# Edge tiles cut at 128 nodes in place of 256, in a graph kernel of three EdgeConv layers and one relational layer

## The chip, the core and the metric

The kernel runs on one core of a Trainium2 chip. TensorE multiplies matrices (PE in the profile, its weight loads PEld), VectorE (DVE) and ScalarE (ACT) work elementwise, GpSimd (POOL) issues indirect DMAs here, SyncE (SP) issues the plain ones. The metric is the device time of one execution in microseconds.

## The reference

A graph of N = 12500 nodes with 128 features and E = 212500 edges (100000 random pairs in both directions and a loop at each node), sorted by their target `dst`. Three EdgeConv layers run one after the other, with a ReLU after the first two:

```python
m = concatenate([x[dst], x[src] - x[dst]])
h = relu(m @ W1 + b1) @ W2 + b2          # one row per edge
x = segment_max(h, dst)                  # -inf becomes 0
```

Then `x = layernorm(x_in + x)`, a relational layer (for each node and each of 8 edge types the mean of the neighbours' rows, times that type's 128x128 matrix, summed over the types, ReLU), and a second residual layernorm.

## The kernel before

`x[dst] @ (W1a - W1b) + b1` is a table in SBUF (`table`, one 128-column block for each 128 nodes, 98 blocks), and `x[src] @ W1b` is a table in DRAM (`tab_b`). An edge needs the sum of one row of each.

**Tiles.** The edges, sorted by target, are cut into tiles of at most 128 edges. A tile never crosses the border of a block of nodes, so each block ends with a tile that is partly empty. In the kernel before a block has 256 nodes (`W2P`, 49 blocks, `NS`), and the number of tiles is a compile-time bound: (E + 49 x 127) / 128 rounded up to a multiple of 16, NT = 1712. Four tiles (`GT`) are a group: 428 groups (`NG`) in each layer, in bodies of eight (`LG`): 53 bodies and a rest of four groups (`OV`). The setup counts the edges of each block, finds each tile's block and first edge, and stores for each tile the target of each edge inside the block (`row_two`), the source (`idx_all`), and the column at which a node's run of edges ends (`col_end`).

**One group** goes through the engines so, eight groups deep on POOL and SP, two deep on the others:
- SP loads `locs` and `cuts` of the group, broadcast to 128 partitions (256 KB, L618).
- POOL gathers the four tiles' source rows from `tab_b`, one indirect DMA a tile (L834). It waits until TensorE is through with the group eight earlier (`s_p1`).
- ScalarE reads the tiles' block numbers and copies each tile's part of `table`, 128x256, to a fixed place (L1270).
- VectorE makes two one-hot matrices of `locs`, against the lanes 0 to 127 (L1564) and 128 to 255 (L1566).
- TensorE, for each tile: a transpose of the gathered rows (L966) and two float32 products of the table's halves with the one-hots, accumulated (L968, two passes each, so four matmuls in the profile). Then W2 for the group before (L975) and four transposes for the one before that (L990).
- ScalarE evicts with ReLU (L1279). VectorE runs a segmented running maximum over the 512 edges of a group (L1593); ScalarE evicts its transposed result (L1291), and SP stores it to `scan_rows` (256 KB, L627).

In layer 0 the position of each node's last edge is found as well: VectorE makes one-hots of the end columns (L1585), TensorE multiplies them with a two-column `lanes` that tells lower from upper half (L982), VectorE collects (L1598). After the last group `end_rows` turns this into `endrow`: comparisons with the tiles' blocks (L1606), two steps on 128x1792 for each half (L1609, L1614), transposes (L1000) and a copy (L1328) for each half, and matmuls that sort by block (L1005). Between layers POOL gathers each node's last row of `scan_rows` by `endrow` (L813), and the tables of the next layer are made.

Beside layer 1's groups VectorE sorts all edges by (source, type), bitonically, with a few passes over 128x2048 between two steps (L1672 and L1673, L1677 and L1678); beside layer 2's it ranks them and cuts them into tiles of the relational stage, and POOL fetches windows. These extra pieces are written into the loops by body number. The relational stage has its own tiles (427 groups, blocks of 256 nodes), gathers from `z_tab` (L891), and is not touched.

Where POOL waits:

```python
for k in range(many):
    at = Lt(l, i, k)
    if at.j == 0:
        pool.wait_ge(s_idx[at.h], at.n + 1)
    pool.wait_ge(s_p1, at.G + 1)
    tick()
    for t in range(GT):
        g.indirect_dma_start(rows[k][:, t, :], None, tab_b, ...
```

Of the kernel before, what the change touches and what calls it, by code (L numbers as in the profile page):

```python
# [24 lines left out]
F32 = mybir.dt.float32  # L25
I32 = mybir.dt.int32
# [19 lines left out]
def gnn_kernel(nc, x, src, dst, etype, params, w_rel, out):  # L46
# [9 lines left out]
    NT = -(-((E + NS * (P - 1)) // P) // HT) * HT  # L56
# [26 lines left out]
    assert NB % CB == 0 and NB + 1 <= P and NB % 2 == 0 and NG % HG == 0 and NG % 2 == 0 and 2 <= OV <= HG  # L83
# [18 lines left out]
    with ExitStack() as ctx:  # L102
# [14 lines left out]
        pidx_up = sb("pidx_up", [P, 1])  # L117
        lane_f = sb("lane_f", [P, 1])
# [37 lines left out]
        thr_row = a.cut(NST)  # L156
        thr_col = a.cut(1, F32, NST)
        jbase = a.cut(NQ)
        full = a.cut(LC * NST).rearrange("p (c b) -> p c b", c=LC)
        cnt0 = a.cut(1, F32, NST)  # L160
        win_at = a.cut(1, I32, NST)
        win_i = a.cut(P, I32, NST)
        win_f = a.cut(P, F32, NST)
        cnt1 = a.cut(1, F32, NST)
        start = a.cut(1, F32, NST)
        step_mat = a.cut(P)
        upto_mat = a.cut(P)
        deg_b = a.cut(1, F32, NS)
        nt_i = a.cut(1, I32, NS)
        nt_f = a.cut(1, F32, NS)  # L170
        upto = a.cut(1, F32, NS)
        shift2 = a.cut(2, F32, NS)
        iota_j = a.cut(NTP, F32, NS)
        past = a.cut(NTP, F32, NS)
# [49 lines left out]
        end_up = a.cut(HT)  # L224
        end_lo = [a.cut(HT) for _ in range(2)]
        lanes = [a.cut(2 * HT, BF16).rearrange("p (t f) -> p t f", f=2) for _ in range(2)]
# [4 lines left out]
        hot_t = [a.cut(2 * GT * P).rearrange("p (h e) -> p h e", h=2) for _ in range(2)]  # L231
        tabs = [a.cut(GT * W2P).rearrange("p (t n) -> p t n", n=W2P) for _ in range(2)]
# [3 lines left out]
        end_at = a.cut(2 * NTP).rearrange("p (f t) -> p f t", f=2)  # L236
        row_base = a.cut(NTP)
        row_t = a.cut(2 * NTP).rearrange("p (f t) -> p f t", f=2)
        blk_hot = a.cut(NQ * NS).rearrange("p (q b) -> p q b", b=NS)
# [149 lines left out]
        s_lane = sem("s_lane")  # L389
# [52 lines left out]
        PV_CONST = 14  # L442
# [336 lines left out]
        def _(pool):  # L779
# [8 lines left out]
            g.iota(thr_row, [[W2P, NST]], base=0, channel_multiplier=0, **exact).then_inc(s_gp, 1)  # L788
            g.iota(thr_col, [[0, 1]], base=0, channel_multiplier=W2P, **exact).then_inc(s_gp, 1)
# [111 lines left out]
        def _(pe):  # L901
# [5 lines left out]
            for c in range(LC):  # L907
                last = mm(ps[0:NST, 0, 0:1], full[:, c, :], ones[:, :], start=(c == 0), stop=(c == LC - 1))
# [1194 lines left out]
```

## Time and profile before

| | |
|---|---|
| time, median of 3 runs | 9480.66 us (9475.42 to 9495.2) |
| the profiled execution | 9484.52 us, span 9482.7 us |
| PE busy | 6710.9 us, 71% |
| PEld busy | 5255.2 us, 55% |
| DVE busy | 5275.8 us, 56% |
| ACT busy | 4898.1 us, 52% |
| POOL busy | 6935.8 us, 73% |
| mean granted TensorE clock | 0.909 |

The three edge layers fill the span from about 145 to 7050 us, the relational stage from about 7286 to the end. A group of instructions is named by its line in the kernel before. Issuing a DMA counts as busy on POOL. The mean of a group of instructions hides where the long ones are, and an engine can be busy for a large share and still always have time in hand: what an engine waited for, and for how long, is read beside it.

### The profile page before, as it was taken

The page shows a single profiled execution, that of the slowest core. Times are in us where ns is not written, and L with a number is a line of the kernel's source. Part 1 is how long each engine was busy: PE and PEld are TensorE (multiplying, and loading weights), DVE is VectorE, ACT ScalarE, POOL GpSimd, SP SyncE. Part 2 cuts the span into 40 slices and gives each one's busy share as a digit, 9 for nine tenths or more (in the row PEclk, how much of TensorE's full clock was granted, in tenths as well). Part 3 has the DMA queues.
Part 4 walks back from the last instruction along what each step waited for, and adds up shares of the span by engine and source line. Part 5 has one row for each costly group of instructions (what it writes and reads, how often), then busy time and mean ns, then how long its engine had stood idle before and what let it go on. Part 6 is the DMA issues. An engine that isn't in the chain of part 4 may idle for free. (4 is left out here: it accounts for less than half of the span.)

```text
span 9482.7 us, 160130 instructions
## 1 busy us (share of the span) xinstructions
PE 6710.9 (71%) x41098; PEld 5255.2 (55%) x41098; DVE 5275.8 (56%) x9611; ACT 4898.1 (52%) x11866; POOL 6935.8 (73%) x7196
## 2 busy tenths in 40 slices
PE   6777777876677777777667777777768555555555
PEld 5666666665565565666555666666654343333333
DVE  5666666665577666666546555555556333333334
ACT  2444444443344444444434444444446777777776
POOL 4777777776777777777777777777764777777775
PEclk9999999998899999999989999999999777777777
DMA  5665656664455555565545666656656222222222
GB/s 144 158 158 157 158 158 158 157 159 126 127 151 148 153 154 153 148 149 149 151 125 147 166 161 162 164 157 157 159 154 248 54 54 54 54 54 54 54 54 67
DMA packets 896156, 1259.78 MB, mean 133 GB/s; under 512 B 185847, under 2 KB 601079, under 8 KB 895270
## 3 DMA queue, kind: packets, MB, share of 16 engines
q1 hardware_dynamic: 650494, 784.23, 27.0%
q0 software_dynamic: 230048, 471.99, 22.6%
q10 hardware_dynamic: 15408, 0.88, 0.1%
q8 instruction: 121, 1.98, 0.1%
q14 instruction: 85, 0.70, 0.0%
HBM read 834.14 MB, written 424.01 MB: 133 GB/s over the span
## 5 line engine op out<-in xcount | busy, mean ns | idle before, releaser
L834 POOL DMA_INDIRECT agg<-tab_b,agg x5136 | 4984.5, 971 | 1596.2 <-issue 1527.3
L968 PE MATMUL ps<-tab_a 128*128 128x128 f32 x20544 | 3080.0, 284 | 3.4 <-issue 3.4
L968 PEld LDWEIGHTS ps<-tab_a 128*128 128x128 f32 x20544 | 2874.6, 202 | 4.1 <-issue 4.0
L966 PE MATMUL ps<-ident,agg 128*128 128x128 f32 x5136 | 1480.8, 288 | 1588.6 <-DMA agg<-tab_b,agg 1503.0
L1593 DVE TENSOR_TENSOR_SCAN agg<-agg,ps 128x512 f32<-128x512 bf16 x1284 | 1639.4, 1277 | 1689.8 <-PE ps L975 1687.7
L1279 ACT ACTIVATE agg<-ps 128x512 f32<-128x512 f32 x1284 | 766.8, 597 | 3475.2 <-PE ps L968 3442.3
L891 POOL DMA_INDIRECT work<-z_tab,work x1708 | 1611.6, 944 | 576.0 <-issue 501.3
L1163 PE MATMUL ps<-tab_a,work 128*128 128x256 f32 x3416 | 1228.0, 522 | 914.7 <-DMA work<-z_tab,work 611.6
L966 PEld LDWEIGHTS ps<-ident,agg 128*128 128x128 f32 x5136 | 753.1, 147 | 1824.6 <-issue 1420.3
L1270 ACT ACTIVATE tab_a<-tab_a 128x256 f32 x5136 | 1713.7, 404 | 52.6 <-issue 41.5
L1163 PEld LDWEIGHTS ps<-tab_a,work 128*128 128x128 f32 x3416 | 841.5, 258 | 1301.3 <-DVE tab_a L2038 1108.2
L2038 DVE TENSOR_TENSOR tab_a<-ps,tab_a 128x256 f32 x1708 | 724.3, 424 | 1416.4 <-PE ps L1163 1230.8
L975 PE MATMUL ps<-agg,w 128*128 128x512 f32 x2568 | 1342.0, 605 | 0.0
L1356 ACT ACTIVATE tab_a<-tab_a,work 128x256 f32<-128x256 f32 x1708 | 883.6, 588 | 467.0 <-PE ps L1163 453.4
L1564 DVE SCALAR_TENSOR_TENSOR tab_a<-agg,pidx,ps 128x512 f32<-128x512 bf16 x1284 | 932.6, 726 | 42.1 <-ACT agg L1279 42.0
L1566 DVE SCALAR_TENSOR_TENSOR tab_a<-agg,pidx_up,ps 128x512 f32<-128x512 bf16 x1284 | 950.0, 740 | 0.0
L990 PEld LDWEIGHTS ps<-ident,agg 128*128 128x128 f32 x5136 | 609.8, 141 | 468.0 <-issue 463.2
L990 PE MATMUL ps<-ident,agg 128*128 128x128 f32 x5136 | 786.5, 276 | 2.5 <-DVE agg L1593 2.3
L1347 ACT ACTIVATE tab_a<-work 128x256 f32<-128x256 f32 x1708 | 727.4, 496 | 62.5 <-ACT tab_a L1356 6.3
L1291 ACT ACTIVATE agg<-ps 128x512 f32<-128x512 f32 x1284 | 739.3, 576 | 16.9 <-PE ps L990 11.5
L1585 DVE TENSOR_SCALAR agg<-iota_b,agg 128x128 bf16<-128x128 bf16 x1712 | 332.9, 271 | 490.3 <-PE ps L982 473.0
L813 POOL DMA_INDIRECT work<-scan_rows,endrow x294 | 288.6, 982 | 197.5 <-issue 99.7
(252 smaller groups left out, 2982.0 us busy)
## 6 DMA issues: line engine op xcount, KB each, us to landing
agg<-row_two SPq DMA_DIRECT2D x1284, 256.0 KB
scan_rows<-agg SPq DMA_DIRECT2D x1284, 256.0 KB
agg<-tab_b,agg POOLq DMA_INDIRECT x5136
z_tab<-tab_a SPq DMA_DIRECT2D x84, 512.0 KB, 3.7
work<-z_tab,work POOLq DMA_INDIRECT x1708, 2.5
tab_b<-work SPq DMA_DIRECT2D x42, 448.0 KB, 3.1
work<-in_x SPq DMA_DIRECT2D x26, 448.0 KB, 5.6
z_tab<-work SPq DMA_DIRECT2D x14, 512.0 KB, 3.9
```

The costliest lines, as they stand in the source:

```text
L834: g.indirect_dma_start(rows[k][:, t, :], None, tab_b, bass.IndirectOffsetOnAxis(ap=idx[at.h][:, at.j * GT + t:at.j * GT + t + 1], axis=0)) ...
L891: g.indirect_dma_start(got[k % LG][:, t, :], None, z_tab, bass.IndirectOffsetOnAxis(ap=meta_of(k, 0, t).bitcast(I32), axis=0)).then_inc(s_ ...
L966: mm(to, rows[at.k][:, t, :], ident[:, :], is_transpose=True, start=True, stop=False)
L968: last = mm(to, tabs[at.s][:, t, h * P:(h + 1) * P], hot_t[at.s][:, h, t * P:(t + 1) * P], start=False, stop=(h == 1))
L975: mm(ps[:, 2 + at.s, :], w2[:, l], h1[at.s], start=True, stop=True).then_inc(s_p2, 1)
L990: last = tr(ps[:, 4 + at.s, t * P:(t + 1) * P], scan[at.s][:, t * P:(t + 1) * P], ident[:, :])
L1163: last = mm(flat[:, to:to + W2P], got[k % LG][:, t, :], hot_r[k % 4][:, t, :], start=True, stop=True)
L1270: last = a_(tabs[s][:, t, :], table[:, bass.ds(blk[t] * W2P, W2P)], ACT.Copy)
L1356: last = a_(hot_r[k % 4][:, t, :], off_r[k % 2][:, t, :], ACT.Relu, scale=meta_of(k, 3, t), bias=meta_of(k, 2, t))
L1564: v.scalar_tensor_tensor(out=hot_t[at.s][:, 0, :], in0=locs[at.k], scalar=pidx[:, 0:1], in1=ps[:, at.s, :], op0=ALU.is_equal, op1=ALU.bypass)
L1566: v.scalar_tensor_tensor(out=hot_t[at.s][:, 1, :], in0=locs[at.k], scalar=pidx_up[:, 0:1], in1=ps[:, at.s, :], op0=ALU.is_equal, op1=ALU.b ...
L1593: v.tensor_tensor_scan(scan[at.s], cuts[at.k], ps[:, 2 + at.s, :], scan[1 - at.s][:, GT * P - 1:GT * P], ALU.min, ALU.max).then_inc(s_scan, 1)
```

## The change

A block has 128 nodes in the edge layers: 98 blocks, and 99 with the end mark. The bound on tiles becomes (E + 98 x 127) / 128 rounded up to a multiple of 16, NT = 1760, 440 groups, 55 bodies and no rest. A target inside its block is now below 128, so one one-hot a group and one float32 product (two matmuls) a tile remain, and ScalarE copies 128x128 a tile. In layer 0 the end marks need one column instead of two, the operations that split the lanes go, and `end_rows` loses its loop over the halves. The setup's operands have 98 or 99 entries in place of 49 or 50. The relational stage keeps blocks of 256.

The core of the diff:

```diff
-    NT = -(-((E + NS * (P - 1)) // P) // HT) * HT
+    NT = -(-((E + NB * (P - 1)) // P) // HT) * HT
...
-        hot_t = [a.cut(2 * GT * P).rearrange("p (h e) -> p h e", h=2) for _ in range(2)]
-        tabs = [a.cut(GT * W2P).rearrange("p (t n) -> p t n", n=W2P) for _ in range(2)]
+        hot_t = [a.cut(GT * P) for _ in range(2)]
+        tabs = [a.cut(GT * P).rearrange("p (t n) -> p t n", n=P) for _ in range(2)]
...
                         mm(to, rows[at.k][:, t, :], ident[:, :], is_transpose=True, start=True, stop=False)
-                        for h in range(2):
-                            last = mm(to, tabs[at.s][:, t, h * P:(h + 1) * P],
-                                      hot_t[at.s][:, h, t * P:(t + 1) * P], start=False, stop=(h == 1))
+                        last = mm(to, tabs[at.s][:, t, :], hot_t[at.s][:, t * P:(t + 1) * P], start=False, stop=True)
...
-                        last = mm(ps[:, 6 + at.h, 2 * col:2 * col + 2], ends[at.s][:, t, :], lanes[at.h][:, col, :],
-                                  start=True, stop=True)
+                        last = mm(ps[:, 6 + at.h, col:col + 1], ends[at.s][:, t, :], lane1[:, :], start=True, stop=True)
...
-                for f in range(2):
-                    for q in range(NQ):
-                        at = f * 2048 + q * P
-                        last = tr(flat[:, at:at + P], end_at[:, f, q * P:(q + 1) * P], ident[:, :])
-                    last.then_inc(s_et, 1)
+                for q in range(NQ):
+                    last = tr(flat[:, q * P:(q + 1) * P], end_at[:, q * P:(q + 1) * P], ident[:, :])
+                last.then_inc(s_et, 1)
                 pe.wait_ge(s_er, 3)
-                for f in range(2):
-                    for q in range(NQ):
-                        last = mm(ps[:, 7, 256 + f * NS:256 + (f + 1) * NS], row_t[:, f, q * P:(q + 1) * P],
-                                  blk_hot[:, q, :], start=(q == 0), stop=(q == NQ - 1))
+                for q in range(NQ):
+                    last = mm(ps[:, 7, 256:256 + NB], row_t[:, q * P:(q + 1) * P], blk_hot[:, q, :],
+                              start=(q == 0), stop=(q == NQ - 1))
...
-                    last = a_(tabs[s][:, t, :], table[:, bass.ds(blk[t] * W2P, W2P)], ACT.Copy)
+                    last = a_(tabs[s][:, t, :], table[:, bass.ds(blk[t] * P, P)], ACT.Copy)
...
-                    for f in range(2):
-                        act.wait_ge(s_et, f + 1)
-                        last = a_(row_t[:, f, :], flat[:, f * 2048:f * 2048 + NTP], ACT.Copy)
-                    last.then_inc(s_er, 3)
+                    act.wait_ge(s_et, 1)
+                    a_(row_t, flat[:, 0:NTP], ACT.Copy).then_inc(s_er, 3)
...
-                    v.scalar_tensor_tensor(out=hot_t[at.s][:, 0, :], in0=locs[at.k], scalar=pidx[:, 0:1],
-                                           in1=ps[:, at.s, :], op0=ALU.is_equal, op1=ALU.bypass)
-                    v.scalar_tensor_tensor(out=hot_t[at.s][:, 1, :], in0=locs[at.k], scalar=pidx_up[:, 0:1],
-                                           in1=ps[:, at.s, :], op0=ALU.is_equal, op1=ALU.bypass).then_inc(s_hot, 1)
+                    v.scalar_tensor_tensor(out=hot_t[at.s], in0=locs[at.k], scalar=pidx[:, 0:1], in1=ps[:, at.s, :],
+                                           op0=ALU.is_equal, op1=ALU.bypass).then_inc(s_hot, 1)
...
-                            v.tensor_scalar(end_up, end_c[at.h], float(P), -float(P), ALU.is_ge, ALU.mult
-                                            ).then_inc(s_lane, 1)
-                            for f, side in enumerate((ALU.is_lt, ALU.is_ge)):
-                                v.tensor_scalar(lanes[at.h][:, :, f], end_c[at.h], float(P), lane_f[:, 0:1], side, ALU.mult)
-                            dve.wait_ge(s_lane, 2 * at.H + 1)
-                            tick()
-                            v.tensor_tensor(end_lo[at.h], end_c[at.h], end_up, ALU.add).then_inc(s_lane, 1)
-                            dve.wait_ge(s_lane, 2 * at.H + 2)
-                            tick()
...
-                    last = v.tensor_scalar(blk_hot[:, q, :], iota[:, 0:NS], blk_col[:, q:q + 1], None, ALU.is_equal)
+                    last = v.tensor_scalar(blk_hot[:, q, :], iota[:, 0:NB], blk_col[:, q:q + 1], None, ALU.is_equal)
...
-                for f in range(2):
-                    last = v.scalar_tensor_tensor(out=row_t[:, f, :], in0=end_at[:, f, :], scalar=0.0, in1=row_base,
-                                                  op0=ALU.is_gt, op1=ALU.mult)
-                last.then_inc(s_ec, 1)
+                v.scalar_tensor_tensor(out=row_t, in0=end_at, scalar=0.0, in1=row_base, op0=ALU.is_gt, op1=ALU.mult
+                                       ).then_inc(s_ec, 1)
```

## Rows read from the trace of the kernel before

**Rows 1.** The page, part 1: busy us of each engine, share, instructions.

```profile
PE 6710.9 (71%) x41098; PEld 5255.2 (55%) x41098; DVE 5275.8 (56%) x9611; ACT 4898.1 (52%) x11866; POOL 6935.8 (73%) x7196
```

**Rows 2.** Windows over L834, one a layer: us, POOL busy, granted clock, DMA share, GB/s.

```profile
144.60:2282.90 2138.30, 1616.71 (x1712) 0.98 0.61 157
2462.20:4710.50 2248.30, 1726.78 (x1712) 0.96 0.57 151
4863.80:7045.10 2181.30, 1641.02 (x1712) 0.96 0.60 158
```

**Rows 3.** Timeline in layer 0: start, us, engine, line, operation [idle before, releaser].

```profile
1002.31 0.30 PE L966 MATMUL ps<-ident,agg 128*128 128x128 f32 x1 [1.33 <-DMA agg<-tab_b,agg]
...
1002.89 0.27 PE L966 MATMUL ps<-ident,agg 128*128 128x128 f32 x1
...
1002.90 0.94 POOL L834 DMA_INDIRECT agg<-tab_b,agg  x1 [0.30 <-issue]
1003.00 0.61 PE L968 MATMUL ps<-tab_a 128*128 128x128 f32 x4
...
1003.45 0.27 PE L966 MATMUL ps<-ident,agg 128*128 128x128 f32 x1
...
1004.15 0.94 POOL L834 DMA_INDIRECT agg<-tab_b,agg  x1 [0.30 <-issue]
...
1005.52 0.64 PE L990 MATMUL ps<-ident,agg 128*128 128x128 f32 x4
```

**Rows 4.** Waits of the whole run: us in total, times, longest.

```profile
ACT agg L1279 <- PE ps L968: 3442.3, 1269, 12.6
...
PE ps L966 <- DMA agg<-tab_b,agg: 1503.0, 1005, 16.1
...
POOL agg L834 <- PE ps L968: 37.2, 122, 0.3
```

**Rows 5.** The page, part 5: two costly groups with count, busy us, mean ns.

```profile
L1270 ACT ACTIVATE tab_a<-tab_a 128x256 f32 x5136 | 1713.7, 404 | 52.6 <-issue 41.5
...
L1566 DVE SCALAR_TENSOR_TENSOR tab_a<-agg,pidx_up,ps 128x512 f32<-128x512 bf16 x1284 | 950.0, 740 | 0.0
```

**Rows 6.** Timeline after layer 0's last gather: the end rows.

```profile
2292.52 2.25 DVE L1606 TENSOR_SCALAR work<-iota,blk_col 128x49 f32<-128x49 f32 x14
...
2294.69 3.95 DVE L1609 SCALAR_TENSOR_TENSOR work<-work 128x1792 f32<-128x1792 f32 x2
...
2302.68 5.43 PE L1000 MATMUL ps<-ident,work 128*128 128x128 f32 x28 [9.64 <-DVE work L1614]
...
2308.22 1.66 ACT L1328 ACTIVATE work<-ps 128x1792 f32<-128x1792 f32 x1 [0.58 <-PE ps L1000]
...
2309.93 11.64 PE L1005 MATMUL ps<-work 128*128 128x49 f32 x56 [1.82 <-ACT work L1328]
...
2323.12 0.94 POOL L813 DMA_INDIRECT work<-scan_rows,endrow  x1 [40.22 <-DVE endrow L1622]
```

**Rows 7.** Layer 1: timeline, then by source line: duration min/median/max ns, first and last start.

```profile
3007.24 1.20 DVE L1677 TENSOR_TENSOR work<-work 128x1024 f32<-128x1024 f32 x1
3007.44 1.82 POOL L834 DMA_INDIRECT agg<-tab_b,agg  x1 [0.31 <-issue]
...
L1672 DVE TENSOR_TENSOR work<-work x110: 658/676/1117, 2535.4 to 2981.5; 128x512 f32<-128x512 f32 x110
...
L1677 DVE TENSOR_TENSOR work<-work x116: 1194/1200/1250, 2999.0 to 4566.2; 128x1024 f32<-128x1024 f32 x116
```

**Rows 8.** The relational stage: L891 by source, and a window (PE, PEld, DVE, ACT, POOL).

```profile
L891 POOL DMA_INDIRECT work<-z_tab,work x1708: 940/944/957, 7285.9 to 9416.8; - x190
...
8000.00:8200.00 200.00, 114.58 (x320) 78.59 (x320) 68.90 (x163) 150.56 (x324) 151.24 (x161) 0.77 0.21 54
```

**Rows 9.** Timeline at the start of layer 2's groups: TensorE.

```profile
4874.06 0.45 PE L966 MATMUL ps<-ident,agg 128*128 128x128 f32 x1 [15.75 <-DMA agg<-tab_b,agg]
...
4875.15 0.42 PE L966 MATMUL ps<-ident,agg 128*128 128x128 f32 x1
```

More of the change, by code:

```diff
@@ L82, in gnn_kernel @@
     assert N + SRC_OFF + P < 16000 and N <= 1 << 14 and R <= 8
-    assert NB % CB == 0 and NB + 1 <= P and NB % 2 == 0 and NG % HG == 0 and NG % 2 == 0 and 2 <= OV <= HG
+    assert NB % CB == 0 and NB + 1 <= P and NB % 2 == 0 and NG % HG == 0 and NG % 2 == 0 and OV in (0, HG)
     TAIL = ERP * P + P - E
@@ L155, in gnn_kernel @@
         last_f = a.cut(LC)
-        thr_row = a.cut(NST)
-        thr_col = a.cut(1, F32, NST)
+        thr_row = a.cut(NBT)
+        thr_col = a.cut(1, F32, NBT)
         jbase = a.cut(NQ)
[L159 to L165, printed above, removed]
+        full = a.cut(LC * NBT).rearrange("p (c b) -> p c b", c=LC)
+        cnt0 = a.cut(1, F32, NBT)
+        win_at = a.cut(1, I32, NBT)
+        win_i = a.cut(P, I32, NBT)
+        win_f = a.cut(P, F32, NBT)
+        cnt1 = a.cut(1, F32, NBT)
+        start = a.cut(1, F32, NBT)
         step_mat = a.cut(P)
         upto_mat = a.cut(P)
[L168 to L174, printed above, removed]
+        deg_b = a.cut(1, F32, NB)
+        nt_i = a.cut(1, I32, NB)
+        nt_f = a.cut(1, F32, NB)
+        upto = a.cut(1, F32, NB)
+        shift2 = a.cut(2, F32, NB)
+        iota_j = a.cut(NTP, F32, NB)
+        past = a.cut(NTP, F32, NB)
         blk_f = a.cut(NQ)
@@ L223, in gnn_kernel @@
         ends = [a.cut(GT * P, BF16).rearrange("p (t n) -> p t n", n=P) for _ in range(2)]
[L224 to L226 removed]
         a = Area(tab_a, TAB)
         table = a.cut((NB + 2) * P)
[L231 to L232 removed]
+        hot_t = [a.cut(GT * P) for _ in range(2)]
+        tabs = [a.cut(GT * P).rearrange("p (t n) -> p t n", n=P) for _ in range(2)]
         a = Area(work, WORK)
[L236 removed]
+        end_at = a.cut(NTP)
         row_base = a.cut(NTP)
[L238 to L239 removed]
+        row_t = a.cut(NTP)
+        blk_hot = a.cut(NQ * NB).rearrange("p (q b) -> p q b", b=NB)
         no_edge = a.cut(NB)
@@ L907, in _ @@
             for c in range(LC):
-                last = mm(ps[0:NST, 0, 0:1], full[:, c, :], ones[:, :], start=(c == 0), stop=(c == LC - 1))
+                last = mm(ps[0:NBT, 0, 0:1], full[:, c, :], ones[:, :], start=(c == 0), stop=(c == LC - 1))
             last.then_inc(s_pt, 1)
             pe.wait_ge(s_pv, PV_START)
-            mm(ps[0:NS, 1, 0:1], step_mat[0:NST, 0:NS], start, start=True, stop=True).then_inc(s_pt, 1)
+            mm(ps[0:NB, 1, 0:1], step_mat[0:NBT, 0:NB], start, start=True, stop=True).then_inc(s_pt, 1)
             pe.wait_ge(s_pv, PV_TILES)
-            mm(ps[0:NS, 2, 0:1], upto_mat[0:NS, 0:NS], nt_f, start=True, stop=True).then_inc(s_pt, 1)
+            mm(ps[0:NB, 2, 0:1], upto_mat[0:NB, 0:NB], nt_f, start=True, stop=True).then_inc(s_pt, 1)
             pe.wait_ge(s_pv, PV_PAST)
@@ L1584, in step @@
                             col = at.j * GT + t
-                            last = v.tensor_scalar(ends[at.s][:, t, :], iota_b[:, :], end_lo[at.h][:, col:col + 1], None,
+                            last = v.tensor_scalar(ends[at.s][:, t, :], iota_b[:, :], end_c[at.h][:, col:col + 1], None,
                                                    ALU.is_equal)
```

49 lines of the change are left out of this document (19 added, 30 removed).

## The prediction

> **What bounds the kernel now.** I began with the page's busy times [rows 1]. POOL has the largest sum and it issues two things only: gathers of rows by index in the three edge layers (L834) and in the relational stage (L891), beside a few at layer ends. TensorE is close behind, so the shares alone do not decide it. The windows over L834, one for each layer from its first gather to its last, do [rows 2]. In layer 0 1712 gathers take 2138.3 us, which is 1.249 us for each, or 4.996 us for a group of four tiles. Layer 1 takes 2248.3 us and layer 2 2181.3 us for the same count. The timeline of one group [rows 3] shows what such an interval is: 0.94 us busy and 0.30 us between two gathers, and the next begins 1.25 us after the last. TensorE in the same stretch stood idle 1.33 us until the gathered rows landed, then worked. The waits say it for the whole run [rows 4]: TensorE waited 1503.0 us for these landings in 1005 places, ScalarE waited 3442.3 us for TensorE, while POOL was held back by TensorE for 37.2 us in 122 places, none over 0.3 us, which is its usual 0.30 us between two gathers. So in the edge layers POOL sets the pace, and TensorE, ScalarE and VectorE all have slack: of its 5.0 us a group takes TensorE about 3.85 us (1002.31 to 1006.16 in rows 3).
>
> **What the change does to each part.** Tiles per layer go from 1712 to 1760, groups from 428 to 440. The three fixed numbers of gathers follow the tiles, whatever the data.
>
> *Term 1, 48 more gathers in each of three layers.* The added groups carry the same four gathers as the others. 48 x 1.249 = 60.0 us in a layer, 179.9 us in three. Nothing hides it, since POOL is the engine that everybody waits for. Each added group also brings its 256 KB load and its 256 KB store on SP's queue; the DMA share is about 0.6 in these windows [rows 2] and the rate per us does not change, so I add nothing for them.
>
> *Term 2, work taken from TensorE, ScalarE and VectorE inside the loops.* Per tile two of four L968 matmuls go. The pitch of a tile is 0.56 us, of which 0.11 us is the transpose's lead (1002.89 to 1003.45 and 1003.00 in rows 3), so the other 0.45 us halves: 0.22 us a tile, 0.89 us a group. VectorE loses one one-hot of 0.74 us a group [rows 5], and in layer 0 the small operations that split the end lanes. ScalarE's copies become half as wide; a 128x128 copy is not in the trace, its cost lies between nothing and the 0.40 us of the 128x256 one [rows 5], and I need no value, because ScalarE waits for TensorE anyway. All of it stands beside POOL's 5.0 us and is worth nothing while the gathers last longer. If that cover were gone these 0.89 us would count; rival A prices it.
>
> *Term 3, the drain after a layer's last gather.* Here no gather follows, and the last group's matmuls are on the path to the store for which the next stage waits. 0.89 us shorter, three times: -2.7 us. Bounds 0 and -5 (two groups' worth and the one-hot).
>
> *Term 4, the end rows after layer 0* [rows 6]. POOL idles 40.2 us here, so every step counts. The 14 comparisons of L1606 go from 49 to 98 columns: 2.25 us now, between 2.25 and 4.5 us then; I take 2.95, +0.7, a third of the way. The two pairs of 1792-column operations (3.95 us for the pair of L1609, and L1614's is like it) become single ones: -3.95. 28 transposes become 14. ScalarE copies their halves one after the other, and the matmuls wait for the second copy, begun at 2308.22 and done at 2309.88; the first, of the same length, begins when half of the 5.43 us and an end of 0.6 us are over, at about 2306.0, and is done at 2307.6: -2.3. The 56 matmuls of L1005 (49 columns, 11.64 us, 0.208 each) become 28 of 98 columns. The nearest row is L1000 with 128 columns in 5.43 / 28 = 0.194, so width costs little there: 28 x 0.208 = 5.8, -5.8 (bounds -5.8 and 0). Sum of the term -11.3 us, bounds -4 and -12.
>
> *Term 5, the sort beside layer 1.* Layer 1 is 110.0 us longer than layer 0 [rows 2], and its POOL busy time is longer by the same 110.1 us (1726.8 against 1616.7), so the gathers themselves last longer. The timeline shows where [rows 7]: VectorE runs a pair of min and max passes over 1024 columns, and the gather that begins inside takes 1.82 us in place of 0.94. There are 55 stages of four shorter passes (L1672 x110 with its partner) and 116 pairs (L1677, L1678). Neither count changes. What a stage costs hangs on where in the gather it starts. From the gathers beside the first of these pairs at 2999.0 us to the last at 4566.2 us, the 116 pairs lose 0.71 us each; starts from 0.15 to 0.30 us after a gather's start lose about 0.05, those 1.1 us after it over 1.5. The passes follow the scan, the scan follows TensorE, and TensorE follows the landing, so the cut of 0.89 us moves all starts. The starts are spread now and I expect them spread then: evenly spread they would lose 0.64 and 0.38 us where they lose 0.71 and 0.42, so -8 and -2: -10 us. The bounds are wide, -110 (none collides) and +70 (most begin at the worst place); both ends would need the starts to lock onto one point. Of the 43 us that layer 2 has over layer 0, 24 are gathers made longer in the same way by the ranking work and the rest eight steps in which POOL fetches windows; no change.
>
> The Trainium skill states this collision as a lock: "SBUF — State Buffer", section "SBUF: two separate sides", has a port pair shared by VectorE and GpSimd that one holds for a whole instruction while the other blocks, for VectorE passes with two SBUF inputs too. The trace agrees (1.82 us in rows 7 against 0.94 in rows 3). By this rule the removed one-hots, which read one operand from PSUM, would free nothing, and the sum stays as it is.
>
> *Term 6, the setup.* 13 comparisons get 99 columns for 50, some small operands 98 or 99 partitions for 49, two small VectorE operations go. VectorE waits for loads around them; 0, bounds -1 and +3.
>
> **Sum.** 179.9 - 2.7 - 11.3 - 10 = +155.9 us. The profiled execution took 9484.5 us for a span of 9482.7: 9640.4. The median of the runs lies 3.9 us below it: 9636.5.
>
> **Rivals.**
>
> A. TensorE is what sets the pace (the other side). If POOL were led by TensorE through the eight buffers, a group would fall from 4.996 us by 0.89 to 4.11 us: 1320 x 4.11 = 5425 us and the 153 us of extra in layers 1 and 2, against 6567.9 us now, so 9484.5 - 990 - 14 = about 8480 us. It decides as soon as a group falls under 4.87 us, where the 12 more groups are paid. For it speaks that TensorE is busy 71% of the span [rows 1]. Against it: the 1005 waits for landings, no wait of POOL above its 0.30 us [rows 4], and the relational stage, where gathers of another table beside other matmuls have the same 0.94 us and the same pace, 161 in 200 us [rows 8]. 3%.
>
> B. The gather itself becomes cheaper with fewer operations of the others beside it. To come out even 156 us in 5280 gathers are needed, 30 ns each of 1249; the time would be about 9480. Against it: a minimum of 940 ns and a median of 944 in the relational stage, where VectorE is busy a third of the time [rows 8], and the same median in the edge layers, so that the other engines seem to cost the gathers nothing outside the sort. 1%.
>
> C. TensorE's clock. Its granted clock is 0.96 to 0.98 in the edge layers [rows 2] and 0.77 in the relational stage [rows 8]. With a quarter of the work taken from it, TensorE waits longer for rows in each group, and the clock will fall to somewhere between. In a stretch at 1.2 GHz, just after 15.75 us of idling, a tile takes 1.09 us in place of 0.56 [rows 9]. A group needs 3.85 - 0.89 = 2.96 us at 2.4 GHz, and 5.9 at most at 1.2, against POOL's 5.0. So it decides only when the granted clock of a whole layer falls under 2.96 / 5.0 = 0.59; at 0.77 a group takes 3.8 us and nothing is lost. At 0.55 it would take 5.4 us, 1320 x 0.39 = 510 us more: about 10,150. 3%.
> The Trainium skill's page "TensorE: Matmul & The Clock Gate", section "HAM oscillation — how this bites in real kernels", speaks against the change here: bursts with waits for DMA between them fall back to half the clock each time. By it alone every group would run at 1.2 GHz and the time go to rival C's; the relational stage, where TensorE waits for gathers too, keeps 0.77 [rows 8], and I go by that.
>
> D. The sort's starts lock. At the two bounds of term 5 the time would be 9537 or 9717 us. For it speaks that all of it is periodic; against it that the delays themselves shift the phase. 5%.
>
> **How the numbers follow.** The forecast, POOL's pace with 48 more gathers a layer, has 88%. The range 9590 to 9675 is 9637 with most of what term 5 leaves open, the rest of the terms together being good for some 10 us. A measurement of this kernel tells 0.2% (19 us) from no change. Forecast, C and D are slower, 96%; B is no change, 1%; A is faster, 3%.
>
> **What would show it.** The L834 windows: 1760 gathers in about 2198 us in layer 0, 2298 in layer 1, 2241 in layer 2, with the median gather still at 0.94 us. TensorE's waits for landings grow by some 1000 us, ScalarE's remain. L968 has 10,560 matmuls. POOL's idle time ahead of the first L813 falls from 40 us to about 28. The granted clock in the edge layers is between 0.77 and 0.96. A layer 0 window under 2180 us, or POOL waiting for TensorE, would make the forecast wrong.

## The result and the profile after

The changed kernel takes 9645.1 us (median of 4, 9638.7 to 9649.7) against 9482.1 us (median of 4), a ratio of 1.017 with a 95% interval of 1.0152 to 1.0187: 163 us slower. 9637 was forecast. Its profiled execution took 9645.8 us, span 9643.9, 161.2 us more than the span before.

The page after, part 1, to be read beside [rows 1], and from part 5 the groups of the gathers and of TensorE's product:

```profile
PE 6280.8 (65%) x31480; PEld 4638.4 (48%) x31480; DVE 4439.2 (46%) x8018; ACT 4500.4 (47%) x12090; POOL 7060.5 (73%) x7340
...
L828 POOL DMA_INDIRECT agg<-tab_b,agg x5280 | 5109.6, 968 | 1645.6 <-issue 1597.4
...
L961 PE MATMUL ps<-tab_a 128*128 128x128 f32 x10560 | 2278.4, 318 | 4.8 <-issue 4.8
```

The same two groups before:

```profile
L834 POOL DMA_INDIRECT agg<-tab_b,agg x5136 | 4984.5, 971 | 1596.2 <-issue 1527.3
...
L968 PE MATMUL ps<-tab_a 128*128 128x128 f32 x20544 | 3080.0, 284 | 3.4 <-issue 3.4
```

TensorE, VectorE and ScalarE all work less, by 430, 837 and 398 us. POOL works 125 us more, and the time follows POOL. The three windows over the gathers (now L828) have the columns of [rows 2]:

```profile
143.70:2342.40 2198.70, 1662.58 (x1760) 0.86 0.59 157
2513.60:4812.30 2298.70, 1762.53 (x1760) 0.85 0.57 151
4964.70:7204.00 2239.30, 1684.43 (x1760) 0.86 0.59 158
```

Layer 0: 2198.7 / 1760 = 1.249 us from one gather to the next, as before. A gather of layer 0 is busy 0.945 us on average (1662.58 / 1760) and was busy 0.944, so the removed one-hots, which read one operand from PSUM, freed nothing. Timeline in layer 0, the place of [rows 3]:

```profile
1000.93 0.94 POOL L828 DMA_INDIRECT agg<-tab_b,agg  x1 [0.30 <-issue]
1001.21 0.44 PE L960 MATMUL ps<-ident,agg 128*128 128x128 f32 x1 [3.29 <-DMA agg<-tab_b,agg]
...
1002.18 0.94 POOL L828 DMA_INDIRECT agg<-tab_b,agg  x1 [0.30 <-issue]
```

TensorE idles 3.29 us ahead of this group where it idled 1.33 us, and finds its clock lower: the transpose takes 0.44 us. Over the run (waits, columns of [rows 4]) its waits for landings grew from 1503 to 2063 us. POOL still idles about 0.30 us ahead of a gather, and in 5122 of 5280 cases (4910 of 5136 before) for "issue", which means nothing that the profile shows:

```profile
ACT agg L1267 <- PE ps L961: 3723.0, 1315, 17.7
...
PE ps L960 <- DMA agg<-tab_b,agg: 2062.6, 882, 21.4
POOL agg L828 <- issue: 1597.4, 5122, 21.6
```

The span, cut at POOL's first and last instruction of each stage (us), also for the experiments told below:

| stage | before | changed | e1 | e2 | e3 | e4 | e7 | e8 | e10 | e13 |
|---|---|---|---|---|---|---|---|---|---|---|
| setup | 144.6 | 143.7 | 142.8 | 145.7 | 145.8 | 144.3 | 144.3 | 143.7 | 145.3 | 143.2 |
| layer 0, gathers | 2138.3 | 2198.8 | 2198.8 | 2139.8 | 2200.9 | 2198.5 | 2199.0 | 2198.6 | 2261.8 | 2200.7 |
| end rows | 40.2 | 26.4 | 36.1 | 25.8 | 28.4 | 29.6 | 26.3 | 27.0 | 27.2 | 27.5 |
| tables for layer 1 | 139.1 | 144.8 | 145.5 | 138.6 | 145.5 | 146.0 | 138.3 | 141.8 | 144.5 | 147.1 |
| layer 1, gathers | 2248.3 | 2298.6 | 2322.4 | 2231.2 | 2283.5 | 2292.8 | 2281.0 | 2299.3 | 2308.8 | 2293.7 |
| border and tables for layer 2 | 153.3 | 152.4 | 154.3 | 153.8 | 154.0 | 156.2 | 155.1 | 153.4 | 151.4 | 154.9 |
| layer 2, gathers | 2181.3 | 2239.3 | 2239.5 | 2181.1 | 2240.7 | 2239.4 | 2241.9 | 2240.6 | 2294.5 | 2243.2 |
| border, up to relational | 240.8 | 242.9 | 248.2 | 242.4 | 244.4 | 243.9 | 243.4 | 243.6 | 244.5 | 243.2 |
| relational and end | 2196.8 | 2197.0 | 2197.7 | 2196.0 | 2196.2 | 2198.0 | 2195.5 | 2195.8 | 2198.1 | 2199.0 |

The changed kernel against before: +168.8 us in the three gather stages, -13.8 in the end rows, +5.7 in the tables for layer 1, the rest +0.5.

The end rows after the change (timeline, lines that answer to [rows 6]):

```profile
2352.15 2.62 DVE L1578 TENSOR_SCALAR work<-iota,blk_col 128x98 f32<-128x98 f32 x14
...
2354.68 2.02 DVE L1580 SCALAR_TENSOR_TENSOR work<-work 128x1792 f32<-128x1792 f32 x1
...
2358.81 3.25 PE L989 MATMUL ps<-ident,work 128*128 128x128 f32 x14 [6.12 <-DVE work L1583]
2362.16 1.66 ACT L1316 ACTIVATE work<-ps 128x1792 f32<-128x1792 f32 x1 [8.78 <-PE ps L989]
2363.87 3.37 PE L993 MATMUL ps<-work 128*128 128x98 f32 x28 [1.81 <-ACT work L1316]
...
2368.79 0.94 POOL L807 DMA_INDIRECT work<-scan_rows,endrow  x1 [26.35 <-DVE endrow L1589]
```

### The profile page after: what moved, and what is told of

Same layout as the page of the kernel before. It is cut to its first block and busy times, and to the rows that moved or that the text cites. A ratio compares the mean times of both kernels' runs of the same rounds, so it can differ in the third digit from the quotient of the medians.

```text
span 9643.9 us, 140435 instructions
## 1 busy us (share of the span) xinstructions
PE 6280.8 (65%) x31480; PEld 4638.4 (48%) x31480; DVE 4439.2 (46%) x8018; ACT 4500.4 (47%) x12090; POOL 7060.5 (73%) x7340
## 5 line engine op out<-in xcount | busy, mean ns | idle before, releaser
L828 POOL DMA_INDIRECT agg<-tab_b,agg x5280 | 5109.6, 968 | 1645.6 <-issue 1597.4
L960 PE MATMUL ps<-ident,agg 128*128 128x128 f32 x5280 | 1686.8, 319 | 2176.1 <-DMA agg<-tab_b,agg 2062.6
L1565 DVE TENSOR_TENSOR_SCAN agg<-agg,ps 128x512 f32<-128x512 bf16 x1320 | 1685.3, 1277 | 2310.1 <-PE ps L967 2308.2
L1267 ACT ACTIVATE agg<-ps 128x512 f32<-128x512 f32 x1320 | 788.1, 597 | 3733.2 <-PE ps L961 3723.0
L961 PE MATMUL ps<-tab_a 128*128 128x128 f32 x10560 | 2278.4, 318 | 4.8 <-issue 4.8
L960 PEld LDWEIGHTS ps<-ident,agg 128*128 128x128 f32 x5280 | 864.3, 164 | 2390.0 <-issue 1386.3
L961 PEld LDWEIGHTS ps<-tab_a 128*128 128x128 f32 x10560 | 1995.9, 235 | 5.6 <-issue 5.4
L967 PE MATMUL ps<-agg,w 128*128 128x512 f32 x2640 | 1660.8, 716 | 2.2 <-issue 2.2
L1258 ACT ACTIVATE tab_a<-tab_a 128x128 f32 x5280 | 1198.3, 297 | 63.0 <-issue 48.4
L981 PEld LDWEIGHTS ps<-ident,agg 128*128 128x128 f32 x5280 | 695.1, 154 | 605.7 <-issue 598.4
L1279 ACT ACTIVATE agg<-ps 128x512 f32<-128x512 f32 x1320 | 774.2, 587 | 319.1 <-PE ps L981 297.2
L981 PE MATMUL ps<-ident,agg 128*128 128x128 f32 x5280 | 880.0, 293 | 5.9 <-DVE agg L1565 3.8
L967 PEld LDWEIGHTS ps<-agg,w 128*128 128x128 f32 x2640 | 515.9, 243 | 2.4 <-issue 2.4
```

The source lines that it names most:

```text
L828: g.indirect_dma_start(rows[k][:, t, :], None, tab_b, bass.IndirectOffsetOnAxis(ap=idx[at.h][:, at.j * GT + t:at.j * GT + t + 1], axis=0)) ...
L960: mm(to, rows[at.k][:, t, :], ident[:, :], is_transpose=True, start=True, stop=False)
L961: last = mm(to, tabs[at.s][:, t, :], hot_t[at.s][:, t * P:(t + 1) * P], start=False, stop=True)
L967: mm(ps[:, 2 + at.s, :], w2[:, l], h1[at.s], start=True, stop=True).then_inc(s_p2, 1)
L981: last = tr(ps[:, 4 + at.s, t * P:(t + 1) * P], scan[at.s][:, t * P:(t + 1) * P], ident[:, :])
L1258: last = a_(tabs[s][:, t, :], table[:, bass.ds(blk[t] * P, P)], ACT.Copy)
```

## The experiments

**e1, e2: the number of tiles alone.** The kernel before with 1760 tiles, and the changed kernel with 1712 (this graph fills 1707 tiles at blocks of 128 and 1684 at 256).

```diff
 # e1, on the kernel before
-    NT = -(-((E + NS * (P - 1)) // P) // HT) * HT
+    NT = -(-((E + NB * (P - 1)) // P) // HT) * HT
...
 # e2, on the changed kernel
-    NT = -(-((E + NB * (P - 1)) // P) // HT) * HT
+    NT = -(-((E + NB // 2 * (P - 1)) // P) // HT) * HT
```

The rest of e1's edit lets ScalarE's loop end on 55 full bodies without a rest, as in the changed kernel.

> The kernel before (blocks of 256, two products a tile) with 1760 tiles a layer, the added 48 being empty. Theory (POOL's gathers set the pace): layer windows over the gathers of 2198, 2308 and 2241 us, the whole 180 us over before, about 9662. The changed kernel is then only 14 to 24 us faster than this one, by its end rows and little else. Rival (work saved on TensorE inside the loops was worth something in the changed kernel): this one is slower than the changed kernel by far more, up to 0.89 us in each of 1320 groups, 1175 us.

> The changed kernel with the number of tiles of before, 1712 (this graph fills 1707 tiles at blocks of 128, so nothing is cut off; for another graph the bound would not hold). Theory: windows of 2138, 2238 and 2180 us and a time 180 us under the changed kernel's, about 9465, so 0.1 to 0.3% under the kernel before. Rival (the empty tiles or the layer's border, not the number of gathers, cost the time): it stays above before.

e1 took 9679.2 us, ratio to before 1.0202 (1.0186 to 1.0217). e2 took 9458.2 us, ratio 0.9967 (0.9955 to 0.9978). Windows over the gathers, first of e1, then of e2:

```profile
142.80:2341.50 2198.70, 1662.61 (x1760) 0.98 0.61 157
2523.10:4845.50 2322.40, 1786.22 (x1760) 0.96 0.56 150
4999.80:7239.20 2239.40, 1684.48 (x1760) 0.96 0.60 158
```

```profile
145.70:2285.50 2139.80, 1618.39 (x1712) 0.86 0.59 157
2449.90:4681.10 2231.20, 1709.82 (x1712) 0.84 0.57 152
4834.90:7016.00 2181.10, 1641.00 (x1712) 0.85 0.59 158
```

Layers 0 and 2 are the same to 2 us in e1 and the changed kernel, and in e2 and before, though TensorE has half of the products in one of each pair. So the number of gathers makes the 60 us a layer, and in these two layers the work saved inside the loops is worth nothing. e1 came out 41 us over the changed kernel in the profiled spans (34 in the medians), where 14 to 24 were expected; 24 of it lie in layer 1, 10 in the end rows and 5 ahead of the relational stage. e2 is faster than both kernels, by 0.33% against before: 14 us from the end rows and 17 from layer 1's window. It holds only for graphs that fill no more than 1712 tiles.

**e3: TensorE's work put back.**

```diff
+                        mm(to, tabs[at.s][:, t, :], hot_t[at.s][:, t * P:(t + 1) * P], start=True, stop=True)
                         mm(to, rows[at.k][:, t, :], ident[:, :], is_transpose=True, start=True, stop=False)
```

> The changed kernel with each tile's product done twice, the first result overwritten, so TensorE has the matmuls of before again while VectorE, ScalarE and the number of tiles stay as changed. Theory: no change, 9640 to 9655, since TensorE works beside the gathers; the granted clock in the edge layers is back at 0.94 to 0.98. Rival (the lower clock of the changed kernel costs time somewhere): it comes out 5 us or more faster although it does more. Rival (TensorE's work counts): 1000 us slower.

It took 9636.3 us (9635.0 to 9641.2), ratio to before 1.0159 (1.0145 to 1.0173), with 10,560 matmuls more. Windows over the gathers of e3:

```profile
145.80:2346.70 2200.90, 1664.92 (x1760) 0.98 0.59 157
2520.60:4804.20 2283.60, 1747.59 (x1760) 0.97 0.57 152
4958.10:7198.90 2240.80, 1686.03 (x1760) 0.96 0.59 158
```

The granted clock is back at 0.96 to 0.98 from 0.85, and layers 0 and 2 do not move. Taken by itself the time of 9 us less would bear out the first rival, that the low clock costs something. The stages say otherwise: no border became shorter, layer 1's window did, by 15 us, and e7 has the same with the low clock. These 15 us lie in the 55 stages of four short passes of the sort: they lose 0.35 us each in e3 and 0.41 in e7, against 0.67 in the changed kernel and 0.57 when it ran again (e13), since they start at other places between two gathers. So neither TensorE's products nor its clock had a part in layers 0 and 2. In layer 1 the time hangs on where the sort's passes start, and code that does nothing (e7) moves that as much as TensorE's products do.

**e4: the sort's passes cut in two.**

```diff
-                    v.tensor_tensor(b_[:, :, 0, :], a_[:, :, 0, :], a_[:, :, 1, :], ALU.min)
-                    last = v.tensor_tensor(b_[:, :, 1, :], a_[:, :, 0, :], a_[:, :, 1, :], ALU.max)
+                    for part in range(2):
+                        if j < 10:
+                            half = SC >> (j + 2)
+                            of_, to_ = (x_[:, part * half:(part + 1) * half] for x_ in (a_, b_))
+                        else:
+                            half = 1 << (j - 1)
+                            of_, to_ = (x_[:, :, :, part * half:(part + 1) * half] for x_ in (a_, b_))
+                        v.tensor_tensor(to_[:, :, 0, :], of_[:, :, 0, :], of_[:, :, 1, :], ALU.min)
+                        last = v.tensor_tensor(to_[:, :, 1, :], of_[:, :, 0, :], of_[:, :, 1, :], ALU.max)
```

> The changed kernel with each of the 116 pairs of 1024-column passes of the sort beside layer 1 written as four passes of 512 columns. Theory (a gather waits for the end of the VectorE pass in progress): a stage then costs what the stages of four short passes cost, 0.42 us in place of 0.71, so layer 1's window falls by about 33 us to 2265, the time to 9612. Rival (a gather waits until the whole stretch of passes is over, or pays by the total time of passes): the window stays at 2298 or grows by a few us.

It took 9645.5 us, with layer 1's window at 2292.7 us: the expectation failed. The 116 stages lose 0.49 us each, as in the changed kernel (0.50). By the start's place they lose 0.1 to 0.5 us, and 1.2 us for starts about 0.55 us after a gather's start, where the long passes lose 0.36. The 55 stages of four short passes lose 1.3 us for starts there in the changed kernel (0.4 in before). That such a gather is held by more than one of the passes is my reading; no row shows which. Shorter passes lowered the worst case of the long ones (1.0 us in the last eighth of the table below, now 0.5) and brought one of their own.

**e10: what makes a VectorE operation hold up a gather.**

```diff
-                    v.scalar_tensor_tensor(out=hot_t[at.s], in0=locs[at.k], scalar=pidx[:, 0:1], in1=ps[:, at.s, :],
+                    v.scalar_tensor_tensor(out=hot_t[at.s], in0=locs[at.k], scalar=pidx[:, 0:1], in1=cuts[at.k],
                                            op0=ALU.is_equal, op1=ALU.bypass).then_inc(s_hot, 1)
```

> The changed kernel with one operand moved: the one-hot's second operand, whose value is not used, is read from the SBUF tile with the cuts in place of PSUM. Same operation, same length, same result. Theory (VectorE passes with two SBUF operands hold up the gathers): one 0.7 us pass a group now meets a gather in about half the cases and costs it 0.33 us on average, so each layer's window grows by 50 to 150 us and the gathers' busy time with it; the kernel comes to 9800 to 10,050. Rival (only the long stretches of the sort do it, by their length): no change, 9645.

It took 9778.0 us (one time; before took 9494.5 beside it). Windows over the gathers, then a one-hot with a gather beginning inside it:

```profile
145.30:2407.10 2261.80, 1725.61 (x1760) 0.84 0.56 153
2578.70:4887.50 2308.80, 1772.63 (x1760) 0.84 0.55 151
5039.00:7333.50 2294.50, 1739.53 (x1760) 0.84 0.55 154
```

```profile
1001.27 0.74 DVE L1549 SCALAR_TENSOR_TENSOR tab_a<-agg,pidx 128x512 f32<-128x512 bf16 x1
1001.61 1.22 POOL L828 DMA_INDIRECT agg<-tab_b,agg  x1 [0.30 <-issue]
```

Layer 0's gathers are busy 63.0 us longer and its window is 63.1 us longer (2198.7 and 1662.58 in the changed kernel). One operand moved from PSUM to SBUF did that, with the same operation and length: 706 of the layer's gathers overlap a one-hot, and they are 63.7 us longer in sum than at 0.944 us each, the 1054 others 0.5 us; in the changed kernel 623 gathers overlap one and are not longer at all. The effect is shown. Its size, 0.14 us a group, is under the 0.17 that I had reckoned, and the 9778 us lie just below the expected band, mainly because layer 1 grew by only 10 us, not 50 or more; why it did is open.

**e5, e6: three gathers a group.**

```diff
-                        for t in range(GT):
+                        for t in range(GT - 1):
                             g.indirect_dma_start(rows[k][:, t, :], None, tab_b,
...
-                    pe.wait_ge(s_rows[at.k], 64 * (at.n + 1))
+                    pe.wait_ge(s_rows[at.k], 48 * (at.n + 1))
...
-                        mm(to, rows[at.k][:, t, :], ident[:, :], is_transpose=True, start=True, stop=False)
+                        mm(to, rows[at.k][:, t % 3, :], ident[:, :], is_transpose=True, start=True, stop=False)
```

> The changed kernel with only three gathers a group; the fourth tile is computed from the rows of the first, so a quarter of the source rows is left out. It takes POOL's 5.0 us a group down to 3.75 and shows what stands behind it. Theory: TensorE needs about 3.0 us at full clock, so POOL still sets the pace, layer 0's window is 440 x 3.75 = 1650 us and the whole about 1600 us shorter, near 8050. Rival (TensorE at its lower clock is the next bound): a group stays above 3.9 us, the window above 1720.

> The kernel before with only three gathers a group, the fourth tile from the rows of the first (a quarter of the source rows left out). Theory: here TensorE's 3.85 us a group and its hand-overs come to the front, so layer 0's window is 428 x 3.9 to 4.3 us = 1670 to 1840 us, above that of the changed kernel with three gathers although it has 12 groups fewer: the work that the change saves is worth something only behind a faster gather. Rival (something other than TensorE and POOL is the next bound, the same in both): the window is 428 x 3.75 = 1605 us, 3% under the changed kernel's.

Both leave out a quarter of the source rows: the fourth tile takes the first one's. e5 took 7995.1 us, e6 7988.1 (one time each). Layer 0 in e5, then in e6 (us; PE, PEld, DVE, ACT, POOL busy; granted clock, DMA share, GB/s):

```profile
144.20:1794.50 1650.30, 1338.06 (x9630) 1004.02 (x9631) 1134.69 (x2740) 899.42 (x2735) 1248.21 (x1320) 0.95 0.70 192
```

```profile
142.50:1748.40 1605.90, 1586.07 (x12740) 1313.87 (x12741) 1439.55 (x3513) 1033.94 (x2654) 1214.79 (x1284) 1.00 0.72 191
```

1650.3 / 440 and 1605.9 / 428 are both 3.75 us: POOL leads in both. For e5 that was expected. For e6 my theory failed: TensorE, at 99% busy and full clock, just keeps up, so its work for a group was less than the 3.85 us I had read. In layer 1, where the sort stands beside it, e6's window is longer, 1801.1 us against 1734.8, but by its gathers and not by TensorE: they are busy 1396.7 us there, e5's 1332.8, though e6 has 36 fewer.

**e11, e12: two gathers a group.** The same edit with `GT - 2`, 32 and `t % 2`, which leaves out half of the source rows.

> The changed kernel with only two gathers a group (half of the source rows left out, tiles 2 and 3 computed from the rows of 0 and 1). POOL could do a group in 2.5 us. With three gathers POOL still led. Theory: TensorE, at about 3.0 us a group at 2.4 GHz, or the hand-overs around it, now leads; layer 0's window is 440 x 3.0 to 3.3 = 1320 to 1450 us. Rival (POOL leads still): 440 x 2.5 = 1100 us.

> The kernel before with only two gathers a group (half of the source rows left out). With three gathers its layer 0 kept POOL's pace of 3.75 us with TensorE busy 99% at full clock. Theory: TensorE leads at about 3.7 us, so layer 0's window stays near 428 x 3.7 = 1590 us, and the changed kernel with two gathers is 150 to 270 us shorter in this layer: here the saved work pays. Rival (the changed kernel's saving never shows, since something common to both leads): both windows are the same per group.

e11 took 6845.8 us, e12 7842.4 (one time each). Layer 0 in e11, in e12, and from e12's waits POOL's longest in total:

```profile
144.40:1356.10 1211.70, 1206.14 (x9577) 957.71 (x9578) 1127.40 (x2723) 887.03 (x2720) 831.86 (x880) 1.00 0.85 236
```

```profile
143.50:1716.00 1572.50, 1567.62 (x12679) 1306.25 (x12680) 1422.01 (x3494) 1029.41 (x2640) 807.62 (x856) 1.00 0.63 177
```

```profile
POOL agg L834 <- ACT agg L1261: 1537.4, 305, 19.0
```

Now TensorE leads in both (99.5% and 99.7% busy), and the change pays: 2.75 us a group against 3.67, 361 us less in this layer, more than the 150 to 270 expected because e11's group was shorter than the 3.0 us that I had put there. POOL, that waited for nobody, now waits 1537 us for the indices that ScalarE hands over behind TensorE. The difference of 0.92 us a group is what the prediction's term 2 gave (0.89).

**e7, e8, e13: a pause with no releaser, and the spread of layer 1.** In the changed kernel POOL stands still 21.61 us before layer 1's first gather, against 15.66 before. The timelines of before, changed, e7 and e8:

```profile
2462.21 0.94 POOL L834 DMA_INDIRECT agg<-tab_b,agg  x1 [15.66 <-issue]
```

```profile
2513.62 0.94 POOL L828 DMA_INDIRECT agg<-tab_b,agg  x1 [21.61 <-issue]
```

```profile
2507.81 0.94 POOL L830 DMA_INDIRECT agg<-tab_b,agg  x1 [15.29 <-issue]
```

```profile
2511.12 0.94 POOL L830 DMA_INDIRECT agg<-tab_b,agg  x1 [17.58 <-issue]
```

```diff
+            for _ in range(16):      # e8: 64
+                tick()
             for l in range(3):
                 if l > 0:
                     for c in range(NC):
```

> The changed kernel with 16 more semaphore increments in POOL's program ahead of its layer loop, which nobody waits for: only the place of all later POOL code moves. It tests the 5.7 us that POOL stands still before layer 1's first gather in the changed kernel (21.6 us idle against 15.7), with no releaser shown. Theory (a stall of POOL's instruction supply that hangs on where the code lies): the idle time ahead of that first gather changes, to 15.7 us or another value, or the stall turns up at another place. Rival (a wait of the changed program, such as a landing that comes later): 21.6 us stays.

> The changed kernel with 64 more semaphore increments ahead of POOL's layer loop. With 16 the pause before layer 1's first gather was gone. Theory (it hangs on where POOL's code lies): the pause is either there as 5.7 us or not, with the rest of the borders equal; layer 1's window falls anywhere between 2275 and 2325 us, as the sort's passes meet the gathers at other points, and these two make up all the difference to the changed kernel. Rival (a steady gain from a later start): the time is 9627 again.

> The changed kernel once more, unchanged, for the spread of one program between executions. Theory: layer 0's and layer 2's windows and the pause of 5.7 us before layer 1's first gather are the same within 2 us; layer 1's window differs by up to some 15 us between executions, and this makes most of the spread of the times. Rival (the alignment of sort and gathers is fixed by the program): layer 1's window is 2298 to 2300 again.

e7 took 9626.9 us (one time), e8 9653.0 (ratio to before 1.0166, 1.0149 to 1.0183), e13 9648.4 (1.0157, 1.014 to 1.0174). POOL's idle time is 21.2 to 23.0 us in the changed kernel, e1, e3, e4, e5, e10, e12 and e13, 18.2 in e6, and 15.3 to 17.6 in before, e2, e7, e8 and e11; e11 has a pause ahead of layer 2's first gather instead (21.1 us, 15.0 to 17.4 in all others). ScalarE waits for the same stores. It begins its copies 0.6 us ahead of POOL in before, e2, e7, e8 and e11, and 6.4 us ahead in the changed kernel (2507.26 us), so a landing that comes late is out. e7 and e8 differ from the changed kernel only in increments for which nobody waits.

The traces show one thing more beside the pause. The DMA queues in the 6.5 us up to layer 1's first gather, in the changed kernel and then in e7:

```profile
q1 hardware_dynamic: 99, 0.67, 28.5%
q14 instruction: 1, 0.01, 0.3%
```

```profile
q1 hardware_dynamic: 948, 0.49, 24.9%
```

In all ten executions with a pause, e6's shorter one and e11's in layer 2 among them, a transfer of 8 KB of the kind "instruction" begins on q14 2.5 to 2.9 us ahead of the late gather (2511.05 us in the changed kernel). Ahead of layer 1's first gather in before, e2, e7, e8 and e11 there is none in the last 8 us. So the reading left, that POOL waits for its own instructions, has the transfer beside it; whose instructions it carries the trace does not say.

The pause is not the time's main lever: e8 lost it and was no faster. e7's 9627 came mostly from layer 1, 2281.0 us against 2298.7, and e8's 2299.3 there answers the rival in its expectation. e13 repeats layer 0 within 2 us; layer 2 differs by 4, where I had expected 2, and layer 1 by 5, less than the 15 I allowed. Its other borders moved by up to 2.5 us.

The next table is about the sort beside layer 1. It sorts the 116 two-pass stages by how long after the start of a gather they start, in eighths of the 1.249 us between gathers, from the timelines of layer 1: the number of stages in each eighth, and their mean loss, by which the gathers beside them exceed 0.944 us.

| eighth | 1 | 2 | 3 | 4 | 5 | 6 | 7 | 8 | sum, us |
|---|---|---|---|---|---|---|---|---|---|
| before, number | 22 | 10 | 13 | 12 | 13 | 17 | 12 | 17 | |
| before, loss | 0.93 | 0.05 | 0.22 | 0.36 | 0.53 | 0.68 | 0.82 | 1.55 | 82.6 |
| changed, number | 16 | 5 | 12 | 39 | 14 | 12 | 7 | 11 | |
| changed, loss | 0.57 | 0.08 | 0.23 | 0.36 | 0.50 | 0.69 | 0.82 | 1.02 | 58.5 |
| e1, number | 15 | 15 | 11 | 8 | 8 | 17 | 13 | 29 | |
| e1, loss | 0.75 | 0.04 | 0.24 | 0.37 | 0.52 | 0.70 | 0.82 | 1.79 | 96.3 |

From the second eighth to the seventh the loss belongs to the place: it is the same in all three. In the first and the last it is not (0.57 to 0.93 us and 1.02 to 1.79). Of the 24 us between before and changed some 12 come from how often a place is hit, reckoned with the losses of before, and 12 from these two eighths. With one product and one one-hot a group the starts gather in the fourth eighth, and the stages with two one-hots and two products hit the last one oftener.

## Why the prediction was right

*What bounds the kernel.* POOL's pace: right, and shown by e1, e2 and e3, which move TensorE's work and the number of gathers apart. Term 1 is the mechanism; that the whole came within 9 us of the forecast is also luck, as terms 3, 4 and 5 show.

*Term 1, +179.9.* The windows of layers 0 and 2 grew by 60.4 and 58.0 us for 60.0 each, layer 1's by 50.4 with term 5 in it. The windows forecast were 2198, 2298 and 2241 us; measured 2198.7, 2298.7 and 2239.3.

*Term 2, nothing from the loops.* Right in sum and in size: the 0.89 us a group are 0.92 where they show (e11 against e12). What was off is TensorE's whole need for a group. I read 3.85 us off one group from first start to last end. The group has no gap, but its end is not where the next can begin: the four transposes at its end take 0.64 us, and when TensorE is in a hurry the next group starts 0.48 us after their start, as these rows of e12 show. 3.67 before and 2.75 after are the need. e6's and e11's expectations failed by it.

```profile
799.98 0.64 PE L990 MATMUL ps<-ident,agg 128*128 128x128 f32 x4
800.46 0.27 PE L966 MATMUL ps<-ident,agg 128*128 128x128 f32 x1
```

*Term 3, the drain, -2.7.* In the profiled execution it came to nothing: +0.1 us after layer 0 (9.6 us from the last gather's end to L1606, 9.7 to L1578), and -0.3 and +0.2 from the last gather's end to the border's first gather at the two others. After layer 0 the last group ran at the lower clock, as this row of the changed kernel's timeline shows:

```profile
2346.68 0.42 PE L960 MATMUL ps<-ident,agg 128*128 128x128 f32 x1
```

That was chance: in e13, the same kernel, it ran at full clock (0.27 us a transpose) and the stretch took 8.1 us, 1.5 less than before. At the two other borders it ran at full clock in the profiled execution as well, and the last scan (L1565) ended 1.5 and 0.9 us sooner after the last gather (6.9 for 8.4, 6.7 for 7.6). What failed there is the path: the matmuls are not what ends last. After layer 1 ScalarE's last eviction waited for an earlier store to land, and after layer 2 POOL's first gather waited for the stores, as it had before (12.13 us idle then):

```profile
4821.05 0.60 ACT L1279 ACTIVATE agg<-ps 128x512 f32<-128x512 f32 x1 [1.92 <-DMA scan_rows<-agg]
...
7216.30 0.94 POOL L807 DMA_INDIRECT work<-scan_rows,endrow  x1 [12.34 <-DMA scan_rows<-agg]
```

*Term 4, the end rows, -11.3.* Measured -14.0 (30.6 us from L1606's start to POOL's first gather, now 16.6). Comparisons +0.4 for +0.7, the 1792-column operations -3.9 as said, transposes and copy -2.2 for -2.3. The term mis-sized is L1005's matmuls, -8.3 for -5.8, and it is their clock: 28 of them take 0.120 us each and not 0.208, but at a granted clock of 1.00, where the 56 of before had 0.53. Windows over them in before, in the changed kernel (L993) and in e13 (us, TensorE's busy time, granted clock, DMA share, GB/s):

```profile
2309.93:2321.57 11.64, 11.64 (x56) 0.53 0.00 0
```

```profile
2363.87:2367.24 3.37, 3.37 (x28) 1.00 0.00 0
```

```profile
2363.77:2369.91 6.14, 6.14 (x28) 0.52 0.00 0
```

In e13, the same kernel once more, they take 0.219 us each at 0.52, and the whole term is -11.2: the forecast at the clock of before. The 2.7 us beyond it are chance. e1's end rows are 4.1 us shorter than those of before with the same code, mainly for this reason: its 56 matmuls had a granted clock of 0.68 and took 9.2 us.

*Term 5, the sort, -10.* Layer 1's gathers are busy 99.9 us longer than layer 0's, 110.1 before. The size is right, the reason half: I expected starts evenly spread at 0.64 us for each of the 116 stages, and they bunched at places that cost 0.50 on average, while the 55 stages of four passes went up from 0.42 to 0.67. Two misses cancelled (-24 and +13 us for -8 and -2), which is luck. e1, e3 and e7 put layer 1 of the same 1760 gathers at 2281 to 2322 us, so a spread of some 40 us belongs to this term, well inside the 180 that I gave as its bounds. By this spread other starts could have put the time some 20 us lower or higher; that is an estimate from these windows.

*Term 6, the setup:* -0.9 us. *Not seen:* the pause of 5.7 us before layer 1's first gather, and 2 us up to the relational stage, for which no run shows a cause.

*The signs.* TensorE's waits for landings grew by 560 us, where I had said some 1000, and ScalarE's waits for TensorE by 281, where I had said that they remain. The halved product took 2278 us for 3080, since TensorE ran slower: its transposes (L960) took 206 us more and W2 (L967) 319 us more than before, with 3% more groups. POOL's idle time ahead of the end rows' first gather fell to 26.4 us, for 28. The windows, the median gather, the 10,560 matmuls and the granted clock came out as said.

*The rivals.* A (TensorE sets the pace) is refuted by e1 and e3; in the kernel before it would hold from about 3.7 us a group down, 1.3 us under POOL's pace (e12). B (cheaper gathers): the median gather is 0.94 us in all kernels. C (the clock): it fell to 0.85, between the 0.77 and 0.96 named, and cost nothing in the loops. Around the end rows it gives and takes up to 3 us between executions of one kernel (terms 3 and 4). It also rose to 1.00 when TensorE was made the bound. The Trainium skill's rule on bursts with waits between them ("TensorE: Matmul & The Clock Gate", section "HAM oscillation — how this bites in real kernels") agrees in direction with the granted 0.85 and not in reach: no layer ran at half the clock throughout. The page's case has bursts shorter than the waits between them; here TensorE needs 2.75 us of a group's 5.0 (e11), so the prediction put the rule to a case that is not its own. D (the starts lock): they bunched, and neither bound was reached.

## What to carry to other kernels

When one engine issues at a fixed interval and all others wait on its results, count its instructions: a change that adds 2.8% to them is paid in full, and what it saves elsewhere is worth nothing until the interval drops to the next engine's need. To find that need, take work from the leader until another one leads; reading it off one group's first start and last end counts the tail over which the next group already starts, 0.2 us of 3.85 here. Where POOL issues gathers, VectorE passes between SBUF tiles beside it cost time by where they meet them, so two variants of such a kernel can differ by tens of us for no reason of their own. A short stretch of matmuls between stages can take 3.4 or 6.1 us in the same kernel, by the clock it meets: read its granted clock before its time is put down to the change.

## What the runs showed that I had not expected

- One unused operand of a VectorE operation, read from SBUF in place of PSUM, cost 63 us in a layer of 440 groups (e10).
- TensorE kept 3.75 us a group at 99% busy (e6) although a group's work had looked like 3.85.
- Halving the length of the passes that hold up the gathers left the loss where it was, 0.49 us a stage (e4).
- Sixteen increments that nobody waits for, ahead of POOL's loops, removed a pause of 6 us (e7), and with it a transfer of 8 KB of instructions.
- The 28 matmuls that sort the end rows took 3.37 us in one execution of the changed kernel and 6.14 in another (e13).
